# A conditioned GRU with residual: reset product in fp16 parts, candidate in 64-column halves, one seed for both gates

## The chip, the cores and the metric

One core of one Trainium2 chip runs the whole kernel. The metric is the device time of one execution in microseconds (us). Before the change it is 2313.37 us, the median of three runs (2312.4 to 2314.2).

## What is computed

A batch of 32 sequences of 512 time steps with 512 features goes through a GRU whose three gates get a constant term from a conditioning vector. Each new state is added to the input at that step.

```
xz, xr, xh = x @ W_z, x @ W_r, x @ W          # for every step, independent of the state
vz, vr, vh = cond @ C_z + b_z, cond @ C_r + b_r, cond @ C + b
step:  z  = sigmoid(xz_t + h @ U_z + vz)
       r  = sigmoid(xr_t + h @ U_r + vr)
       hh = tanh(xh_t + (r * h) @ U + vh)
       h  = (1 - z) * h + z * hh
out = x + h_t for every t
```

All arrays are fp32 with 512 x 512 weights. The 512 steps are a chain: step t needs the state of step t-1 twice in sequence, once for r and once more, through r, for hh.

## The kernel before, in words

**Layout.** A 32 x 512 tile (batch x features) lies as 128 partitions x 128 columns: partition block j of 32 partitions holds feature columns 128 j to 128 j + 127. VectorE's transpose in 32 x 32 blocks of such a tile gives the operand that TensorE loads as weights: 32 columns of it are the 32 batch rows for one of four groups q of 128 features. A product with a 512 x 512 matrix is four values of q times four column tiles j, 16 matmuls of 128 x 32 weights and 128 moving columns. The four of one q go to different column tiles of the array. An fp32 matmul shows as two records in the trace, each with its weight load.

**fp16 parts.** Where a product isn't done in fp32, both operands are scaled by a power of two and split in a high and a low fp16 part; three of the four products of parts are taken (`PARTS`). So it is with x @ W (`project`: 12 groups of four matmuls with 384 columns, all three gates at once) and h @ U_z (`update_product`, L253: 48 matmuls of 128 columns). h @ U_r and (r * h) @ U are fp32 (`product`, L225: 16 matmuls, 32 records each).

**One step on TensorE** (`step`, L299), in program order: the reset product R from the transposed state `h_t`, half by half as it comes; the update product U from `h_hi` and `h_lo`; in every fourth step a total of |x| (`total_x`), which gives the scale of a coming set of four steps; the first three groups (`BEFORE_C`) of the projection for step s+2; the candidate product C from `reset_t`, again half by half; the other nine groups. The projection has its own bank, one for even and one for odd steps. Waits, and so the order of everything, are written out by hand; each engine has its own program with semaphores.

**The seeds.** Before a product the cell in PSUM gets its starting value from VectorE: projection times scale plus constant term (`seed`, L441, one operation for each gate), and the matmuls add to it. For this the bits that make a matmul add must be set; six matmuls with zeros (L285) do that once. There are two sets of three cells, for even and odd steps. U_z is scaled, so the update cell's seed and constant are scaled as well and ScalarE's sigmoids take the scale back (`z_down`, `z_minus`, read from memory).

**The other engines in a step.** ScalarE: `h_hi` (L366), sigmoid for r (L368), the two sigmoids of z (L370, L371), tanh (L373), and at the end of three steps in four an operation on x for a later set: sum of |x|, fp32 scaling, high part (`sum_x`, `whole_x`, `high_x`). VectorE: seed of R for step s+1, `h_lo` (L523), reset times state and its transpose in two halves of 64 columns (L533, L535), seeds of the update and the candidate for s+1, transposition of x (L438), `taken` = z * hh (L549), new state and its transpose in two halves (L553, L555). GpSimd: `kept` = (1 - z) * h, low part of x, and the addition of x for the output. SyncE moves x and out in blocks of eight steps.

**Loops.** TensorE loops over sets of four steps and has the last 11 steps unrolled (L321 to L325). ScalarE, VectorE and GpSimd loop over 64 steps; ScalarE runs a one-element sigmoid at the head of its loop (L398), ahead of which stands the loading of its table.

**Ahead of the steps** the weights W_r, W_z, W_h and U_z are each measured, scaled and split (`top_of_w`, `rest_of_w`), the constant terms are computed with the C weights in fp32, and the loop starts when U_r and U_h have arrived too.

## Time and profile before

| | |
|---|---|
| median of three runs | 2313.37 us |
| time of the profiled execution | 2313.02 us |
| its span, first to last instruction | 2311.1 us |
| TensorE matmul busy | 2260.8 us, 98% |
| TensorE weight loads busy | 1885.7 us, 82% |
| VectorE busy | 1743.3 us, 75% |
| ScalarE busy | 1036.7 us, 45% |
| GpSimd busy | 686.8 us, 30% |
| chain that ended last, by engine | PE 96% |

PE is TensorE's matmul side and PEld its weight loads, which overlap it; DVE is VectorE, ACT ScalarE, POOL GpSimd. Times of rows are from the start of the span. A matmul's row gives its latency; matmuls are pipelined, so the pace is read from the starts of consecutive ones or from the pieces of the chain. A group's bracket gives the idle time of its engine ahead of it and what ended it.

### The profile page before, as it was taken

The page shows a single profiled execution, that of the slowest core. Times are in us where ns is not written, and L with a number is a line of the kernel's source. Part 1 is how long each engine was busy: PE and PEld are TensorE (multiplying, and loading weights), DVE is VectorE, ACT ScalarE, POOL GpSimd, SP SyncE. Part 2 cuts the span into 40 slices and gives each one's busy share as a digit, 9 for nine tenths or more (in the row PEclk, how much of TensorE's full clock was granted, in tenths as well). Part 3 has the DMA queues.
Part 4 walks back from the last instruction along what each step waited for, and adds up shares of the span by engine and source line. Part 5 has one row for each costly group of instructions (what it writes and reads, how often), then busy time and mean ns, then how long its engine had stood idle before and what let it go on. Part 6 is the DMA issues. An engine that isn't in the chain of part 4 may idle for free.

```text
span 2311.1 us, 185969 instructions
## 1 busy us (share of the span) xinstructions
PE 2260.8 (98%) x82966; PEld 1885.7 (82%) x82966; DVE 1743.3 (75%) x7717; ACT 1036.7 (45%) x3091; POOL 686.8 (30%) x1546
## 2 busy tenths in 40 slices
PE   3999999999999999999999999999999999999998
PEld 2888888888888888888888888888888888888887
DVE  5777777777777777777777777777777777777776
ACT  3444444444444444444444444444444444444443
POOL 0333333333333333333333333333333333333332
PEclk9999999999999999999999999999999999999999
DMA  9110110110110110101101101101101011011001
GB/s 192 33 37 22 33 37 19 37 37 19 37 37 19 37 34 21 37 23 33 37 19 37 37 18 37 37 19 37 34 22 37 24 32 37 19 37 37 19 19 22
DMA packets 145367, 78.25 MB, mean 34 GB/s; under 512 B 9024, under 2 KB 140608, under 8 KB 145216
## 3 DMA queue, kind: packets, MB, share of 16 engines
q1 hardware_dynamic: 145216, 76.84, 13.8%
q14 instruction: 131, 1.07, 0.2%
q8 instruction: 20, 0.33, 0.1%
HBM read 43.25 MB, written 33.55 MB: 33 GB/s over the span
## 4 chain that ended last, share of the span: by engine, by line
PE 96%; SPq 2%; issue 1%; DMA 1%; ACT 0%; DVE 0%; ACTq 0%; POOLq 0%; POOL 0%; DVEq 0%
PE p_bank L238 43%; PE banks L230 39%; PE banks L260 15%; SPq L136 1%; DMA u<-in_L_cond_U_dram 1%; SPq L131 0%; PE p_bank L246 0%; SPq L146 0%; SPq L139 0%; ACT h_hi L366 0%; ACT table L398 0%; ACTq L397 0%; ACT L398 0%; ACT gate_c L373 0%; POOLq L48 0%
## 5 line engine op out<-in xcount | busy, mean ns | idle before, releaser
L238 PE MATMUL p_bank<-w_hi,x_t 128*32 128x384 f16 x16384 | 1189.1, 327 | 3.6 <-DVE w_lo L465 3.5
L238 PE MATMUL p_bank<-w_lo,x_t 128*32 128x384 f16 x8192 | 712.1, 327 | 0.0
L238 PEld LDWEIGHTS p_bank<-w_hi,x_t 128*32 128x32 f16 x16384 | 482.6, 97 | 144.4 <-issue 4.0
L230 PE MATMUL banks<-u,h_t 128*32 128x128 f32 x16352 | 544.9, 274 | 5.8 <-DMA u<-in_L_cond_U_dram 4.1
L230 PE MATMUL banks<-u,reset_t 128*32 128x128 f32 x16352 | 541.6, 273 | 1.4 <-issue 0.9
L230 PEld LDWEIGHTS banks<-u,h_t 128*32 128x32 f32 x16352 | 411.4, 109 | 107.7 <-DVE h_t L555 93.6
L200 POOL TENSOR_TENSOR kept<-keep,state 128x128 f32<-128x128 f32 x512 | 234.4, 458 | 887.3 <-ACT keep L370 887.3
L230 PEld LDWEIGHTS banks<-u,reset_t 128*32 128x32 f32 x16352 | 428.5, 109 | 82.8 <-DVE reset_t L535 66.5
L443 DVE SCALAR_TENSOR_TENSOR banks<-p_bank,x_down,base 128x128 f32<-128x128 f32 x1536 | 478.4, 342 | 4.2 <-issue 3.8
L212 POOL TENSOR_TENSOR result<-x_nat,state 128x128 f32<-128x128 f32 x512 | 234.2, 457 | 723.0 <-DVE state L553 723.0
L533 DVE TENSOR_TENSOR reset<-gate_r,state 128x64 f32<-128x64 f32 x1024 | 209.3, 204 | 210.6 <-ACT gate_r L368 210.5
L366 ACT ACTIVATE h_hi<-h_t 128x128 f16<-128x128 f32 x512 | 158.3, 309 | 398.1 <-DVE h_t L555 398.1
L373 ACT ACTIVATE gate_c<-banks 128x128 f32<-128x128 f32 x512 | 141.9, 277 | 398.7 <-PE banks L230 398.7
L549 DVE TENSOR_TENSOR taken<-gate_c,gate_z 128x128 f32<-128x128 f32 x512 | 149.4, 292 | 185.0 <-ACT gate_c L373 185.0
L535 DVE STREAM_TRANSPOSE reset_t<-reset 128x64 f32<-128x64 f32 x1024 | 251.7, 246 | 37.5 <-DVE reset L533 1.7
L238 PEld LDWEIGHTS p_bank<-w_lo,x_t 128*32 128x32 f16 x8192 | 241.2, 97 | 47.3 <-issue 0.3
L555 DVE STREAM_TRANSPOSE h_t<-state 128x64 f32<-128x64 f32 x1024 | 251.2, 245 | 35.3
L370 ACT ACTIVATE keep<-banks,z_minus 128x128 f32<-128x128 f32 x512 | 188.1, 367 | 190.6 <-PE banks L260 190.6
L368 ACT ACTIVATE gate_r<-banks 128x128 f32<-128x128 f32 x512 | 141.8, 277 | 245.4 <-PE banks L230 245.2
L187 POOL TENSOR_TENSOR x_parts<-x_whole,x_parts 128x128 f16<-128x128 f32 (+1 forms) x509 | 237.0, 466 | 8.4 <-ACT x_parts L339 8.4
L553 DVE TENSOR_TENSOR state<-taken,kept 128x64 f32<-128x64 f32 x1024 | 208.5, 204 | 17.4
L260 PE MATMUL banks<-uz_hi,h_hi 128*32 128x128 f16 x8176 | 208.6, 219 | 0.5
(55 smaller groups left out, 1869.8 us busy)
## 6 DMA issues: line engine op xcount, KB each, us to landing
x_nat<-in_x_dram SPq DMA_DIRECT2D x256, 128.0 KB, 3.0
out_dram<-result SPq DMA_DIRECT2D x256, 128.0 KB, 2.7
w_stage<-in_L_cond_W_r_dram SPq DMA_DIRECT2D x4, 256.0 KB, 5.6
w_stage<-in_L_cond_W_z_dram SPq DMA_DIRECT2D x4, 256.0 KB, 8.4
w_stage<-in_L_cond_W_dram SPq DMA_DIRECT2D x4, 256.0 KB, 10.8
u<-in_L_cond_U_z_dram SPq DMA_DIRECT2D x4, 256.0 KB, 13.6
c_w<-in_L_cond_C_r_dram SPq DMA_DIRECT2D x4, 256.0 KB, 12.3
c_w<-in_L_cond_C_z_dram SPq DMA_DIRECT2D x4, 256.0 KB, 15.2
```

The costliest lines, as they stand in the source:

```text
L187: return nc.gpsimd.tensor_tensor(x_parts[k][:, part_of, 1], x_whole[k][:, part_of], x_parts[k][:, part_of, 0], ALU.subtract)
L200: nc.gpsimd.tensor_tensor(kept[:], keep[:], state[:, (tt - 1) % SLOTS], ALU.mult).then_inc(kept_ready, 1)
L212: nc.gpsimd.tensor_tensor(result[o][:, t], x_nat[j % BUFS][:, t], state[:, tt % SLOTS], ALU.add)\
L230: last = nc.tensor.matmul(out[part(j)], turned[:, part(q)], weights[:, q, cols(j)], start=first and q == 0, stop=q == Q - 1, skip_group_ch ...
L238: last = nc.tensor.matmul(p_bank[k][part(j), 0:G * N], x_t[:, c, part(q), a], w[b][:, :, q, cols(j)], start=f == 0, stop=f == GROUPS - 1, ...
L260: last = nc.tensor.matmul(out[part(j)], (h_hi, h_lo)[a][:, part(q)], uz[b][:, q, cols(j)], start=False, stop=q == Q - 1, skip_group_check= ...
L370: nc.scalar.activation(keep[:], cell(k, Z), ACT.Sigmoid, scale=z_minus[:]).then_inc(z_keep, 1)
L443: last = V.scalar_tensor_tensor(cell(k, g), p_bank[k][:, cols(g)], x_down[d][:, g:g + 1], base[:, g], ALU.mult, ALU.add)
L533: V.tensor_tensor(reset[:, half(a)], gate_r[:, half(a)], old[:, half(a)], ALU.mult).then_inc(reset_ready, 1)
L535: V.transpose(reset_t[:, half(a)], reset[:, half(a)]).then_inc(reset_t_ready, 1)
L553: V.tensor_tensor(new[:, half(a)], taken[:, half(a)], kept[:, half(a)], ALU.add).then_inc(h_ready, 1)
L555: V.transpose(h_t[:, half(a)], new[:, half(a)]).then_inc(h_t_ready, 1)
```

## The change

1. *Reset product in fp16 parts.* U_r is split like U_z (`ur_hi`, `ur_lo`). The product is 48 matmuls, taken by halves of the state: high parts of half 0 (two weight parts), low part of half 0, the same for half 1. `h_hi` and `h_lo` are computed in two halves each. The reset sigmoid runs in two halves and reads its scale from memory.
2. *Scales.* W_r and W_z share one scale, U_z and U_r another, W_h has its own. U_r is loaded before the biases, where it was loaded behind the C weights.
3. *One seed for both gates.* The cells of reset and update are in neighbouring banks and get one seed of 256 columns, behind the reset transposes. The candidate has one pair of banks for all steps, one for each half of its columns, seeded within its own step behind `h_lo` (`seed_c`).
4. *Candidate by halves of its output columns* (`candidate_product`): columns 0 to 63 of each block first, with one projection group between the two operand halves, then columns 64 to 127. Two groups of the projection lie ahead of it instead of three. Each half has its own tanh, `taken`, new state and transpose; VectorE's order is take 0, renew 0, take 1, turn 0, renew 1, turn 1.
5. *Waits and loops.* TensorE waits for the candidate's seed before the projection; GpSimd's output addition waits for the next step's `h_lo`. Step 1 on TensorE is unrolled ahead of the loop and waits for U_h only before its candidate product; the last 10 steps are unrolled. ScalarE's first four steps are unrolled, and its loop edge comes after every fourth step of a 64-step pass.

The diff, cut to its core:

```diff
-        banks = [ctx.enter_context(nc.psum_tensor(f"banks{k}", [P, G, BANK], f32)) for k in range(2)]
+        banks = [ctx.enter_context(nc.psum_tensor(f"banks{k}", [P, GATES, BANK], f32)) for k in range(2)]
+        c_bank = ctx.enter_context(nc.psum_tensor("c_bank", [P, HALVES, BANK], f32))
...
             load_weights(u[:, Z], U_z, s_u_in[Z])
+            load_weights(u[:, R], U_r, s_u_in[R])
...
             load_x(1, 1)
-            load_weights(u[:, R], U_r, s_u_in[R])
...
                 pool.wait_ge(h_ready, HALVES * (s + 1) if first or last else pool.snap(HALVES * s + HALVES))
+                if not (last and tt == STEPS - 1):
+                    pool.wait_ge(h_lo_ready, HALVES * (s + 2) if first or last else pool.snap(HALVES * s + 2 * HALVES))
...
+            def candidate_product(halves, between):
+                for a in range(HALVES):
+                    for h in range(HALVES):
+                        if a == 0:
+                            pe.wait_ge(*halves[h])
+                        for q in range(Q // HALVES * h, Q // HALVES * (h + 1)):
+                            for j in range(J):
+                                last = nc.tensor.matmul(c_bank[part(j), a, 0:N // HALVES], reset_t[:, part(q)],
+                                                        u[:, C, q, half_cols(j, a)], start=False, stop=q == Q - 1,
+                                                        skip_group_check=True)
+                        if (a, h) == (0, 0):
+                            between()
+                    last.then_inc(c_mm, 1)
...
+            def reset_product(out, halves):
+                passes = [(h, a, b) for h in range(HALVES) for a in range(2) for b in range(2 - a)]
+                for n, (h, a, b) in enumerate(passes):
+                    if b == 0:
+                        pe.wait_ge((h_hi_ready, h_lo_ready)[a], halves[h])
+                    for q in range(Q // HALVES * h, Q // HALVES * (h + 1)):
+                        for j in range(J):
+                            last = nc.tensor.matmul(out[part(j)], (h_hi, h_lo)[a][:, part(q)], ur[b][:, q, cols(j)],
+                                                    start=False, stop=n == len(passes) - 1 and q == Q - 1,
+                                                    skip_group_check=True)
+                return last
...
-                product(cell(k, R), h_t, u[:, R], halves=[(h_t_ready, a) for a in halves]).then_inc(r_mm, 1)
-                update_product(cell(k, Z), now).then_inc(z_mm, 1)
+                reset_product(cell(k, R), halves).then_inc(r_mm, 1)
+                update_product(cell(k, Z)).then_inc(z_mm, 1)
+                pe.wait_ge(c_seeded, now)
...
-                    project(k, (c + 2) % SET, 0, BEFORE_C)
-                product(cell(k, C), reset_t, u[:, C], halves=[(reset_t_ready, a) for a in halves]).then_inc(c_mm, 1)
+                    project(k, (c + 2) % SET, 0, BEFORE_C - 1)
+                if candidate_in is not None:
+                    pe.wait_ge(candidate_in, 16 * J)
+                def one_group():
+                    if fill:
+                        project(k, (c + 2) % SET, BEFORE_C - 1, BEFORE_C)
+                candidate_product([(reset_t_ready, a) for a in halves], one_group)
                 if fill:
                     project(k, (c + 2) % SET, BEFORE_C, GROUPS)
+            step(0, 1, True, s_u_in[C])
             with pe.Fori(0, SETS - 3) as m:
-                for tt in range(1, SET + 1):
+                for tt in range(2, SET + 2):
                     step(m, tt, False)
...
+                for a in range(HALVES):
+                    act.wait_ge(h_t_ready, HALVES * s + (a + 1) if first or last else act.snap(HALVES * s + (a + 1)))
+                    nc.scalar.activation(h_hi[:, half(a)], h_t[:, half(a)], ACT.Copy, scale=2.0 ** POW)\
+                        .then_inc(h_hi_ready, 1)
                 act.wait_ge(r_mm, now)
-                nc.scalar.activation(gate_r[:], cell(k, R), ACT.Sigmoid).then_inc(r_gate, 1)
+                for a in range(HALVES):
+                    nc.scalar.activation(gate_r[:, half(a)], banks[k][:, R, half(a)], ACT.Sigmoid, scale=gates_down[:])\
+                        .then_inc(r_gate, 1)
...
+                for a in range(HALVES):
+                    act.wait_ge(c_mm, HALVES * s + (a + 1) if first or last else act.snap(HALVES * s + (a + 1)))
+                    nc.scalar.activation(gate_c[:, half(a)], c_bank[:, a, 0:N // HALVES], ACT.Tanh).then_inc(c_gate, 1)
...
+            for tt in range(SET):
+                step(0, tt, False, True)
             with nc.Fori(0, PASSES - 1, engines=[act.engine], hint_back_edge=True) as i:
-                nc.scalar.activation(table[:], z_minus[:], ACT.Sigmoid)
-                for tt in range(STEPS):
+                nc.scalar.activation(table[:], gates_minus[:], ACT.Sigmoid)
+                for tt in range(SET, STEPS + SET):
                     step(i, tt, False)
...
+            def seed_gates(k, d):
+                V.scalar_tensor_tensor(banks[k][:, :, 0:N], p_bank[k][:, 0:GATES * N].rearrange("p (g n) -> p g n", g=GATES),
+                                       x_down[d][:, W_GATES:W_GATES + 1], base[:, 0:GATES], ALU.mult, ALU.add)\
+                    .then_inc(seeded, 1)
+            def seed_c(k, d):
+                V.scalar_tensor_tensor(c_bank[:, :, 0:N // HALVES], in_halves(p_bank[k][:, cols(C)]),
+                                       x_down[d][:, W_C:W_C + 1], in_halves(base[:, C]), ALU.mult, ALU.add)\
+                    .then_inc(c_seeded, 1)
...
+                for a in range(HALVES):
+                    dve.wait_ge(h_hi_ready, count(HALVES * s + (a + 1)))
+                    V.scalar_tensor_tensor(h_lo[:, half(a)], h_t[:, half(a)], 2.0 ** POW, h_hi[:, half(a)], ALU.mult,
+                                           ALU.subtract).then_inc(h_lo_ready, 1)
+                seed_c(tt % 2, m % 2)
...
+                take(0)
+                renew(0)
+                take(1)
+                turn(0)
+                renew(1)
+                turn(1)
```

## Rows read from the trace of the kernel before

**Rows 1.** The page's first part: busy time, share of the span, instructions.

```profile
PE 2260.8 (98%) x82966; PEld 1885.7 (82%) x82966; DVE 1743.3 (75%) x7717; ACT 1036.7 (45%) x3091; POOL 686.8 (30%) x1546
```

**Rows 2.** The chain of waits, 1001 to 1020: start us, us, what.

```profile
1003.52 0.05 PE p_bank L246 x7
...
1006.42 0.88 PE banks L230 x32
1007.30 0.67 PE banks L260 x48
1007.97 0.49 PE p_bank L238 x12
1008.45 0.87 PE banks L230 x32
1009.33 1.46 PE p_bank L238 x36
```

**Rows 3.** Timeline of one step: start us, us, engine, line, operation.

```profile
1007.36 0.28 ACT L368 ACTIVATE gate_r<-banks 128x128 f32<-128x128 f32 x1 [0.47 <-PE banks L230]
...
1007.67 0.22 DVE L533 TENSOR_TENSOR reset<-gate_r,state 128x64 f32<-128x64 f32 x1 [0.39 <-ACT gate_r L368]
...
1007.78 0.35 PE L238 MATMUL p_bank<-w_hi,x_t 128*32 128x384 f16 x4
...
1007.93 0.24 DVE L535 STREAM_TRANSPOSE reset_t<-reset 128x64 f32<-128x64 f32 x1
...
1008.01 0.37 ACT L370 ACTIVATE keep<-banks,z_minus 128x128 f32<-128x128 f32 x1 [0.37 <-PE banks L260]
```

**Rows 4.** Timeline of a late step without projection.

```profile
2298.81 0.24 DVE L535 STREAM_TRANSPOSE reset_t<-reset 128x64 f32<-128x64 f32 x1
...
2299.11 1.08 PE L230 MATMUL banks<-u,reset_t 128*32 128x128 f32 x32 [0.26 <-DVE reset_t L535]
```

**Rows 5.** Timeline: one-column fp32 matmuls, then the projection.

```profile
1003.35 0.22 PE L246 MATMUL p_bank<-x_sum,row_sum 128*32 128x1 f32 x8
...
1003.41 0.34 PE L238 MATMUL p_bank<-w_hi,x_t 128*32 128x384 f16 x4
```

**Rows 6.** Groups by line and form: busy us, mean ns, idle before.

```profile
L370 ACT ACTIVATE keep<-banks,z_minus 128x128 f32<-128x128 f32 x512 | 188.1, 367 | 190.6 <-PE banks L260 190.6
...
L366 ACT ACTIVATE h_hi<-h_t 128x128 f16<-128x128 f32 x512 | 158.3, 309 | 398.1 <-DVE h_t L555 398.1
...
L339 ACT ACTIVATE x_parts<-x_nat,x_up 128x512 f16<-128x512 f32 x128 | 112.1, 876 | 0.0
...
L398 ACT ACTIVATE table<-z_minus 128x1 f32<-128x1 f32 x7 | 1.4, 203 | 0.1
```

**Rows 7.** Timeline of a loop edge of ScalarE and VectorE.

```profile
333.00 1.28 ACT L398 ACT_TABLE_LOAD   x1 [0.37 <-issue]
...
334.40 0.29 ACT L366 ACTIVATE h_hi<-h_t 128x128 f16<-128x128 f32 x1
334.51 0.36 DVE L443 SCALAR_TENSOR_TENSOR banks<-p_bank,x_down,base 128x128 f32<-128x128 f32 x1 [0.63 <-issue]
...
334.75 0.23 PEld L260 LDWEIGHTS banks<-uz_hi,h_hi 128*32 128x32 f16 x16 [0.39 <-ACT h_hi L366]
```

**Rows 8.** Queues with instructions, all of them, 76 to 2250: packets, MB, share.

```profile
q14 instruction: 126, 1.03, 0.2%
```

**Rows 9.** The same from 2254 to 2304, queue q8.

```profile
q8 instruction: 13, 0.21, 1.9%
```

**Rows 10.** Windows of four looped and of 11 unrolled steps: busy (instructions), clock.

```profile
1001.80:1019.35 17.55, 17.55 (x656) 14.71 (x652) 13.46 (x61) 7.95 (x24) 5.36 (x12) 1.00 0.24 60
2254.10:2304.60 50.50, 47.25 (x1668) 40.29 (x1664) 33.70 (x150) 17.48 (x56) 13.03 (x29) 1.00 0.07 15
```

**Rows 11.** Waits from 2254 to the end: us, times, longest.

```profile
PEld banks L230 <- issue: 5.9, 13, 1.7
```

**Rows 12.** Timeline: TensorE's first step in the recurrence.

```profile
55.63 1.93 PE L230 MATMUL banks<-u,h_t 128*32 128x128 f32 x32 [4.11 <-DMA u<-in_L_cond_U_dram]
```

More of the change, by code:

```diff
@@ L279, in _ @@
                 pe.wait_ge(s_c_in[g], 16 * J)
-                product(cell(1, g), cond_t, c_w[:, g], first=True).then_inc(s_base_mm, 1)
-            pe.wait_ge(s_zeros, 1)
+                product(base_cell(g), cond_t, c_w[:, g], first=True).then_inc(s_base_mm, 1)
             pe.wait_ge(s_base, G)
-            for k in range(2):
-                for g in range(G):
-                    nc.tensor.matmul(banks[k][:, g], zeros[:, 0:P], zeros[:], start=True, stop=True).then_inc(s_bits, 1)
+            clear_bits(c_bank)
+            clear_bits(banks[1])
             pe.wait_ge(seeded, 1)
+            pe.wait_ge(c_seeded, 1)
             pe.sem_inc(r_mm, 1)
             pe.sem_inc(z_mm, 1)
-            pe.sem_inc(c_mm, 1)
+            pe.sem_inc(c_mm, HALVES)
             total_x(TOTAL_STEP % 2, 0, 0, 3)
@@ L293, in _, with step @@
             project(0, 2, 0, GROUPS)
-            pe.wait_ge(s_w_hi, G + 1)
-            pe.wait_ge(s_w_lo, G + 1)
-            for g in range(G):
-                pe.wait_ge(s_u_in[g], 16 * J)
-            def step(m, tt, last):
+            def step(m, tt, last, candidate_in=None):
                 s = m * SET + tt
@@ L351, in _ @@
             high_x(1)
-            for m, g in enumerate(SPLITS):
-                act.wait_ge(s_w_up, m + 1)
-                nc.scalar.activation(split_of(g, 0), stage_of(g), ACT.Copy, scale=w_up[:, g:g + 1]).then_inc(s_w_hi, 1)
+            for g in SPLITS:
+                k = SCALE_OF[g]
+                act.wait_ge(s_w_up, k + 1)
+                nc.scalar.activation(split_of(g, 0), stage_of(g), ACT.Copy, scale=w_up[:, k:k + 1]).then_inc(s_w_hi, 1)
+            nc.scalar.activation(table[:], w_up[:, 0:1], ACT.Sigmoid)
             act.wait_ge(x_in[1], 16 * J)
@@ L514, in more @@
                     return not (last and m + sets >= STEPS // SET)
-                ahead = (tt + 1) % 2, (tt + 1) // SET % 2
-                if not (last and tt == STEPS - 1):
-                    if t == SET - 1:
-                        dve.wait_ge(x_down_ready, count(now_m + 2))
-                    dve.wait_ge(projected, count(s + 2))
-                    seed(*ahead, (R,))
-                dve.wait_ge(h_hi_ready, now)
-                V.scalar_tensor_tensor(h_lo[:], h_t[:], 2.0 ** POW, h_hi[:], ALU.mult, ALU.subtract)\
-                    .then_inc(h_lo_ready, 1)
-                if t == POWER_STEP and more(2):
+                for a in range(HALVES):
[3 more added lines that the diff above has]
+                seed_c(tt % 2, m % 2)
+                if t == POWER_STEP and more(2):
+                    dve.wait_ge(projected, count(s + 2))
                     power_x(m % 2, p_bank[TOTAL_STEP % 2][:, G * N:G * N + 1], now_m + 2, count)
@@ L539, in step @@
                 if not (last and tt == STEPS - 1):
[L540 removed]
+                    if t == SET - 1:
+                        dve.wait_ge(x_down_ready, count(now_m + 2))
+                    dve.wait_ge(projected, count(s + 2))
+                    seed_gates((tt + 1) % 2, (tt + 1) // SET % 2)
                 if t == POWER_STEP and more(2):
```

175 lines of the change are left out of this document (100 added, 75 removed).

## The prediction

> **What bounds the kernel now.** I read the busy shares first: TensorE is busy 98% of the span, VectorE 75% [rows 1]. The reader is to see that only TensorE can be the bound by its own work. Next the chain of waits of a step: it stays on TensorE throughout, in five pieces: reset product R 0.88 us, update product U 0.67, three projection groups 0.49, candidate product C 0.87, nine projection groups 1.46, together 4.37 us; one step in four has the total of x besides, 0.05 [rows 2]. The mean step is thus 4.385, and 511 steps are 2241 of the 2311 us span. Then the order of time within a step: what must happen between the end of R and the start of C on the other engines, since this runs beside U and three groups [rows 3]. In these rows the first transpose of `reset` ends at 1008.17, and C starts at about 1008.27, when the three groups have issued (1007.78 + 0.49). So the chain through the engines is only some 0.04 us shorter than its cover once TensorE's reaction is added. The kernel is bound by TensorE, with a recurrence just under it.
>
> **The change, part by part.**
>
> *R in half precision.* Thirty-two fp32 records (0.88) become 48 fp16 matmuls of the shape of U's: 0.67. Saves 0.21 a step.
>
> *C in 64-column halves.* The 32 records of 128 columns become 64 of 64 columns. No row has that shape. The fp16 product of 128 columns starts 48 matmuls in 0.67, that is 0.056 us for each four (one per column tile), and the fp32 product of 128 columns 0.109 for each four [rows 2]. Half the columns of the latter are the stream of the former: 16 x 0.056 = 0.89, plus 0.02. Bounds: if halving saved nothing, 16 x 0.109 = 1.74; and no less than 0.87, since the same columns pass. I take 0.89, because the one-column fp32 matmuls lie far under it: eight start in 0.06, 0.03 for each four [rows 5], so neither issue nor weight load holds the pairs at 0.056.
> A rule speaks against this part. The Trainium skill (TensorE: Matmul & The Clock Gate, "Wait — 56ns, not 53.3ns?") has a floor of about 25 ns from one matmul's start to the next, however few columns. By it C would be 64 x 0.025 = 1.6. The trace has 14 ns in U and under 8 ns in the one-column rows, so it disagrees where matmuls go to different column tiles.
>
> *TensorE's own sum* is 0.67 + 0.67 + 0.33 (two groups) + 0.89 + 0.16 (the group moved into C) + 1.46 = 4.18, against 4.37.
>
> *The cover of the reset chain shrinks.* Two groups instead of three lie ahead of C. Cover after R: 0.67 + 0.33 = 1.00. The chain: ScalarE starts 0.23 after the last fp16 matmul's successor has started (1007.78 to 1008.01) [rows 3]; the half gate; 0.03; reset 0.23; 0.03; transpose 0.24; 0.06 to TensorE (2299.05 to 2299.11, a step in which TensorE really waits) [rows 4]. The half gate now has its scale from memory. Such an activation of 128 columns takes 0.367 and of one column 0.203 [rows 6]; without it 128 columns take 0.28 [rows 3]. Bounds 0.20 and 0.37; I take 0.30, midway in columns and a little up. Sum 1.12: TensorE waits 0.12 before every C (0.02 to 0.19 by the bounds). In the steps with the total the wait is 0.07. The transposed second half comes 0.38 after the first; C's first quarter and the group in between last 0.22 + 0.16, so it is just in time.
>
> *Step: 4.18 + 0.13 = 4.31.* Gain 0.075 a step.
>
> *Back half, hidden.* From C's start TensorE has 0.89 + 0.16 + 1.46 = 2.51 until the next R. First columns complete after 0.61; tanh of a half (as the gate without a scale, 0.28, less 64 columns: 0.22) starts at 0.84, second at 1.28 and ends at 1.50; `take(1)` starts at 1.53 and sits ahead of `turn(0)` on VectorE, which ends at 1.93; h_hi's half (0.309 for 128 columns [rows 6]; 0.24) and TensorE's reaction bring R's operand at 2.27. Slack 0.24. ScalarE's work on x sits between (it starts at 1.39; the longest takes 0.88 [rows 6]): at most 2.47, still inside. R's later operand halves (h_lo after VectorE's two short operations) come before TensorE needs them. If this cover went, each 0.1 over costs 51 us.
>
> *VectorE.* Three seeds become two: one of 256 columns, estimated 0.48, one of 128 at 0.35 (a seed takes 0.36 [rows 7]); two operations are split (h_lo, taken), about 0.08 each. Sum about level with before. The candidate's seed moves behind h_lo, beside the rest of R; the gates' seed behind the reset. Neither ends last: `take(0)` is ready at 1.09 after C's start and VectorE is free at 1.03. With both ends of the seed (0.36 to 0.72) the cost is 0 to 0.02 a step. GpSimd's new wait for h_lo delays its addition by 0.6 us of 4.3, with nothing behind it before `keep`.
>
> *Loop edges.* ScalarE's loop edge has a table load: load at 333.00, h_hi only at 334.40, and U waits 0.39 [rows 7]. The next h_hi is now R's own operand. Tanh's end to the load 0.37, load 1.28, 0.12, h_hi 0.24, 0.06: 2.07 after 1.50 is 3.57 against the 2.51 available, a wait of 1.05 at 6 edges, +6.3 (before about 0.3 each, inside its total). VectorE's edge shows 0.63 of "issue" ahead of a seed [rows 7]; now h_lo stands there: about 0.5 x 7 = +3.5. Together 10.
>
> *Instructions fetched.* TensorE's queue q8 brings code: 13 packets, 0.21 MB, while the last, unrolled steps ran 1,664 pairs [rows 9, 10], so 64 B an instruction and 256 in a packet; none in the whole loop, where q14 alone loads instructions, for other engines [rows 8]. Those 13 packets took 50.5 us, 3.9 each; without the 5.9 us in which TensorE stood for "issue" there [rows 11] it is 3.4. A step now has 208 pairs, was 160: 256 instructions are 2.6 us of work, less than a packet's 3.4 to 3.9. So where code is new, code sets the pace. The end: 10 unrolled steps, 3,990 instructions, 15.6 packets x 3.75 (nearer the end at which it stood) = 58.5 us instead of 43 of work. The start: 8.2 packets for the unrolled step and the loop's first pass, between 21.6 (work alone) and 32 (8.2 x 3.9); I take 27.5.
>
> **Sum**, from the start of step 1 (55.63) [rows 12] to TensorE's end (2304.6): before 2249. After: 27.5 + 124 passes x 4 x 4.31 (2138) + 10 + 58.5 = 2234, 15 less. The start itself stays: U_r comes ahead of the C weights and delays the base by some 4 us, but the first R no longer waits for U_h; I take 0, bounds -3 and +3. Span 2311.1 - 15 = 2296; the profiled execution's time is 1.9 over its span: 2298. It was 2313.0 before, 0.4 under the median.
>
> **The rivals.**
> - *Wait absent.* If the half gate costs 0.20 to 0.22, the wait before C is 0.03 and the step 4.22: 0.09 x 511 = 46 less, 2252. For: one-column gates take 0.203. Against: 128 columns take 0.367.
> - *Reset chain longer (slower).* At 0.367 for the half gate the wait is 0.19 and the step 4.38, no gain, and the edges and code (+25) are then on top: 2335. It decides from 0.06 us more anywhere between R's end and the transposed half. For: the chain was within 0.04 of its cover already. Against: halves of other operations are shorter here.
> - *The loop's code no longer stays (slower).* The body grows from 1,313 to about 1,697 instructions, 84 to 109 KB; the trace shows only that 84 KB stay. From its place in the program it touches seven 16 KB blocks and ends within a few instructions of an eighth. If the block at the head is lost on each pass, TensorE stands about 3 us (a packet, 3.4 to 3.9, less what is queued) at 124 edges: +370, 2668. The Trainium skill (Advanced Engine Details and Errata, "ISA Cache") gives TensorE 128 KB in lines of 16 KB, eight lines: by it seven blocks and the one fetched ahead just fit, and one more would not.
> - *A floor per matmul (slower).* If the starts of the short fp32 records and not their columns set the pace, halving saves nothing: C takes 1.74, 511 steps 434 us more, 2732. The one-column rows speak against it [rows 5]. By the skill's 25 ns (TensorE: Matmul & The Clock Gate) it would be 1.6, and 2660.
>
> **How the numbers follow.** Forecast 60%, own range 2275 to 2322 (half gate 0.26 to 0.33, packet 3.4 to 3.9). Wait absent 8%, longer chain 15%, code lost 14%, floor 3%. The range 2250 to 2345 holds the first three and leaves out the last two and some tails. What a measurement can tell is 0.2%, 4.6 us. Under 2308.7: 45 of the 60 and the 8, 0.53. Within: 9 and 3, 0.12. Above: 6, 12, 14 and 3, 0.35.
>
> **What would show it.** R's piece 0.67 and C's with its group 1.05; every step 4.31, the ones with the total too. TensorE idle 0.12 before C, released by `reset_t`, some 60 us in sum. No wait at R except at loop edges (about 1 us, ScalarE). q8 packets about 9 up to the loop's end and 15 behind it, none between; packets within the loop mean the code rival. R waiting on h_hi or h_lo in every step would make the prediction wrong, and so would a half gate far from 0.30.

## The result: slightly slower

| | before | after |
|---|---|---|
| median | 2313.47 us (8 runs, 2312.4 to 2315.6) | 2319.92 us (8 runs, 2319.1 to 2322.0) |
| span of the profiled execution | 2311.1 us | 2318.3 us |

The ratio after to before is 1.0028, 95% interval 1.0017 to 1.0039: 6.5 us slower, just beyond what can be told from no change. Forecast was 2298, faster. The time lies in the forecast's own range (2275 to 2322), with the other sign. One of the four executions of experiment 4 took 4600 us, the other three 2403 to 2405; it is not in that experiment's ratio.

The page's first part and its instruction queues, of the kernel after [rows 1, 8]:

```profile
PE 2241.4 (97%) x107502; PEld 1815.9 (78%) x107502; DVE 1799.7 (78%) x8226; ACT 1295.2 (56%) x4623; POOL 687.6 (30%) x1546
...
q8 instruction: 26, 0.43, 0.1%
```

TensorE has 24,536 more matmuls and is busy 19 us less; ScalarE has 1,532 more instructions and is busy 259 us more. Nothing but TensorE is near a bound. Next the chain of waits of one steady step after (start us, us, what), against [rows 2]:

```profile
1006.75 0.67 PE banks L298 x48
1007.42 0.67 PE banks L307 x48
1008.09 0.33 PE p_bank L270 x8
1008.42 0.38 PE c_bank L259 x16
1008.80 0.16 PE p_bank L270 x4
1008.96 0.67 PE c_bank L259 x48
1009.63 1.46 PE p_bank L270 x36
```

R has fallen from 0.88 to 0.67 as it should. But the candidate's first quarter, 16 matmuls, takes 0.38 in the chain where the next 48 take 0.67 (0.22 for 16): a wait hides in it. From the starts of the matmuls, as a median over some 410 steps, the pieces are 0.670, 0.670, 0.462, 0.248, 0.162, 0.672 and 1.462: 4.346 a step, against 4.375 before (means of all but the long steps: 4.346 after, 4.391 before). The timeline after shows the wait (start, length, engine, line, operation, in brackets the engine's idle time ahead and what ended it), against [rows 3]:

```profile
1007.24 0.41 PE L307 MATMUL banks<-uz_hi,h_hi 128*32 128x128 f16 x16
...
1007.47 0.52 ACT L429 ACTIVATE gate_r<-banks,gates_down 128x64 f32<-128x64 f32 x2 [0.80 <-PE banks L298]
...
1007.81 0.22 DVE L615 TENSOR_TENSOR reset<-gate_r,state 128x64 f32<-128x64 f32 x1 [0.56 <-ACT gate_r L429]
...
1008.07 0.24 DVE L617 STREAM_TRANSPOSE reset_t<-reset 128x64 f32<-128x64 f32 x1
...
1008.37 0.27 PEld L259 LDWEIGHTS c_bank<-u,reset_t 128*32 128x32 f32 x16 [0.34 <-DVE reset_t L617]
```

From U's first matmul to C it is 1.13 us, against a forecast of 1.12, and the cover is the forecast's 1.00. Now the whole run. I take the start of U in steps 6 and 501 as marks; the chain before and after, in that order:

```profile
79.96 0.67 PE banks L260 x48
...
2255.23 0.67 PE banks L260 x48
```

```profile
76.90 1.34 issue
...
81.19 0.70 issue
...
85.80 0.67 PE banks L307 x48
...
2246.85 0.67 PE banks L307 x48
```

After is 5.8 us late at step 6, 8.4 ahead at step 501, and 7.2 late at the end. So the loop did bring 14.2 us; the first steps took 6.0 of them, and the last eleven 15.6. Within the loop seven steps are long, six of them 64 apart by 1.44 to 1.63 each and one by 0.79, 9.9 in sum. Before has six long steps too, 64 apart, but by 0.23 to 0.29 only, 1.5 in sum. Without the long steps the gain is 495 x (4.391 - 4.346) = 22. The first long one after, against [rows 7]:

```profile
338.46 0.36 DVE L603 SCALAR_TENSOR_TENSOR h_lo<-h_t,h_hi 128x64 f16<-128x64 f32 x2 [1.65 <-issue]
...
338.74 0.29 PE L298 MATMUL banks<-ur_hi,h_lo 128*32 128x128 f16 x8 [1.33 <-DVE h_lo L603]
```

VectorE stands 1.65 us for its own instructions, and R stands with it. ScalarE's edge has no table load any more, only the small activation that is there to hold the table, and R doesn't wait:

```profile
355.36 0.20 ACT L463 ACTIVATE table<-gates_minus 128x1 f32<-128x1 f32 x1 [0.44 <-issue]
```

The end after: the chain with its pieces of "issue", then a window over the last ten steps (us, busy and instructions of PE, PEld, DVE, ACT, POOL, granted clock, DMA share, GB/s) against [rows 10], and the queue there against [rows 9]:

```profile
2269.47 0.70 issue
2270.17 0.68 PE banks L298 x34
...
2272.65 1.12 issue
...
2276.72 1.07 issue
```

```profile
2250.50:2312.30 61.80, 44.50 (x1988) 38.08 (x1984) 31.35 (x143) 20.87 (x78) 11.66 (x26) 0.95 0.07 13
...
q8 instruction: 16, 0.26, 1.9%
```

TensorE works 44.5 of 61.8 us. Of the other 17, the list of waits puts 15.8 down to "issue", and 1.5 to operands in the last steps. Sixteen packets of 256 instructions come meanwhile, so I read "issue" as waiting for code; experiment 5 tests it.

### The profile page after: what moved, and what is told of

It reads as the page before. It is cut to its first block, busy times and chain, and to the rows that moved or that the text cites. A ratio compares the mean times of both kernels' runs of the same rounds, so it can differ in the third digit from the quotient of the medians.

```text
span 2318.3 us, 238050 instructions
## 1 busy us (share of the span) xinstructions
PE 2241.4 (97%) x107502; PEld 1815.9 (78%) x107502; DVE 1799.7 (78%) x8226; ACT 1295.2 (56%) x4623; POOL 687.6 (30%) x1546
## 4 chain that ended last, share of the span: by engine, by line
PE 95%; issue 2%; SPq 1%; DMA 1%; DVE 0%; ACT 0%; DVEq 0%; POOLq 0%; POOL 0%
PE p_bank L270 43%; PE c_bank L259 23%; PE banks L298 15%; PE banks L307 15%; SPq L152 1%; DMA x_nat<-in_x_dram 1%; PE p_bank L279 0%; SPq L147 0%; SPq L163 0%; DVE taken L637 0%; DVE state L641 0%; ACT gate_c L436 0%; DVE h_t L645 0%; SPq L155 0%; DVE h_lo L603 0%
## 5 line engine op out<-in xcount | busy, mean ns | idle before, releaser
L259 PEld LDWEIGHTS c_bank<-u,reset_t 128*32 128x32 f32 x32704 | 506.7, 110 | 213.7 <-DVE reset_t L617 164.4
L259 PE MATMUL c_bank<-u,reset_t 128*32 128x64 f32 x32704 | 648.9, 221 | 9.4 <-issue 9.0
L429 ACT ACTIVATE gate_r<-banks,gates_down 128x64 f32<-128x64 f32 x1024 | 265.9, 310 | 426.0 <-PE banks L298 425.3
L298 PE MATMUL banks<-ur_hi,h_lo 128*32 128x128 f16 x8176 | 303.4, 219 | 9.2 <-DVE h_lo L603 8.4
L298 PE MATMUL banks<-ur_hi,h_hi 128*32 128x128 f16 x8176 | 303.4, 219 | 2.3 <-issue 1.2
L298 PE MATMUL banks<-ur_lo,h_hi 128*32 128x128 f16 x8176 | 303.5, 219 | 0.7 <-issue 0.7
L425 ACT ACTIVATE h_hi<-h_t 128x64 f16<-128x64 f32 x1024 | 251.9, 250 | 92.0 <-DVE h_t L645 58.3
L603 DVE SCALAR_TENSOR_TENSOR h_lo<-h_t,h_hi 128x64 f16<-128x64 f32 x1024 | 229.6, 225 | 71.3 <-ACT h_hi L425 21.7
L270 PEld LDWEIGHTS p_bank<-w_lo,x_t 128*32 128x32 f16 x8192 | 242.1, 97 | 50.8 <-issue 5.1
L637 DVE TENSOR_TENSOR taken<-gate_c,gate_z 128x64 f32<-128x64 f32 x1024 | 229.9, 225 | 40.0 <-ACT gate_c L436 15.6
L507 DVE SCALAR_TENSOR_TENSOR banks<-p_bank,x_down,base 128x256 f32<-128x256 f32 x512 | 235.9, 461 | 0.0
```

The costliest lines, as they stand in the source:

```text
L259: last = nc.tensor.matmul(c_bank[part(j), a, 0:N // HALVES], reset_t[:, part(q)], u[:, C, q, half_cols(j, a)], start=False, stop=q == Q - ...
L270: last = nc.tensor.matmul(p_bank[k][part(j), 0:G * N], x_t[:, c, part(q), a], w[b][:, :, q, cols(j)], start=f == 0, stop=f == GROUPS - 1, ...
L298: last = nc.tensor.matmul(out[part(j)], (h_hi, h_lo)[a][:, part(q)], ur[b][:, q, cols(j)], start=False, stop=n == len(passes) - 1 and q == ...
L425: nc.scalar.activation(h_hi[:, half(a)], h_t[:, half(a)], ACT.Copy, scale=2.0 ** POW)\
L429: nc.scalar.activation(gate_r[:, half(a)], banks[k][:, R, half(a)], ACT.Sigmoid, scale=gates_down[:])\
L507: V.scalar_tensor_tensor(banks[k][:, :, 0:N], p_bank[k][:, 0:GATES * N].rearrange("p (g n) -> p g n", g=GATES), x_down[d][:, W_GATES:W_GAT ...
```

## The experiments

Twelve kernels, all against the kernel before on the same chip. Ratios are to before with their 95% interval; after has 1.0028. Before's median was 2313.5 beside after and 2312.1 to 2313.4 beside the experiments, so a difference to after of 1 us or so says nothing. First the table by stretches, each from the starts of U in the profiled execution (start of U in step 1 to step 6; to step 501, with the sum of its long steps' excess in brackets and the mean of the others; to the end of the trace):

```
                      median   1 to 6   6 to 501 (long)  mean step  last 11
before                2313.5    22.4     2175.2 (1.5)      4.391      56.1
after                 2319.9    28.4     2161.1 (9.9)      4.346      71.7
four groups ahead     2277.8    29.5     2118.8 (10.3)     4.259      69.4
none between          2318.3    28.4     2160.5 (9.9)      4.345      69.5
gate without scale    2275.6    30.5     2117.2 (10.9)     4.255      68.7
candidate whole       2404.8    26.4     2257.7 (7.0)      4.547      60.9
longer loop           2303.5    29.4     2160.4 (9.9)      4.345      54.3
VectorE written out   2309.3    29.0     2150.5 (0)        4.345      70.5
R in fp32             2343.2    26.8     2194.0 (6.1)      4.420      61.0
before, longer loop   2310.2    23.6     2175.1 (1.5)      4.391      52.7
three edits           2249.3    29.5     2108.0 (0)        4.259      53.1
turn first            2332.1    30.8     2189.2 (0)        4.423      54.3
two seeds             2311.8    28.1     2154.1 (2.8)      4.346      68.6
three, two seeds      2252.7    30.8     2110.4 (0)        4.264      53.8
```

**1. Four groups ahead of the candidate.**

```diff
-    BEFORE_C = 3
+    BEFORE_C = 4
```

> Four of the twelve projection groups stand ahead of the candidate's product instead of three (one of the four still between its operand halves, eight behind it). Theory A (TensorE's 0.137 us of waiting per step in the changed kernel is for the first half of reset_t, which VectorE ends too late): the fourth group is 0.16 us of work that fills the wait, so the step falls from 4.346 to about 4.21 us, 496 steps bring 65 us, and the time is about 2255 us (2245 to 2270). The price: the part behind the candidate is 0.16 us shorter, so its slack of about 0.24 us falls to about 0.1; R should still not wait, save in steps with x's own splitting on ScalarE. Theory B (the period of the loop is set by the chain from the candidate back to R, which gets no shorter by a longer cover): the wait moves ahead of R, the step stays at 4.33 to 4.35 us and the time at 2312 to 2320 us.

2277.8 us, ratio 0.985 (0.983 to 0.987): 42 us less than after. The chain of a step, and TensorE's waits from 100 to 2200 us (us in total, times, longest):

```profile
1006.36 0.73 PE banks L298 x48
1007.10 0.67 PE banks L307 x48
1007.76 0.49 PE p_bank L270 x12
1008.25 0.23 PE c_bank L259 x16
```

```profile
PEld banks L298 <- ACT h_hi L425: 86.7, 374, 0.3
PEld c_bank L259 <- DVE reset_t L617: 69.6, 369, 0.2
```

The wait ahead of C is gone, 16 matmuls take 0.223. The kernel after has in the same stretch

```profile
PEld c_bank L259 <- DVE reset_t L617: 157.5, 481, 0.4
```

What stands here at 69.6 is the ordinary gap of the weight loads, since the matmuls behind it start without a break. Theory A holds in kind. It gave 65 us and 42 came. The whole 0.162 of C's place came back, but R now waits 0.025 before its first matmul and 0.036 inside: `h_hi`, 86.7 us in the waits. And in one step in four the total of x costs its 0.06, which the wait had hidden. That leaves 0.087 a step. The kernel after has no such row for `h_hi` there: its nine groups covered it.

What had cost C's first quarter 0.025 shows in the weight loads. Here the first one starts ahead of its matmul (this is a step with the total of x), where in the step of after shown above it starts with it:

```profile
1003.75 0.32 PEld L259 LDWEIGHTS c_bank<-u,reset_t 128*32 128x32 f32 x16
...
1003.84 0.40 PE L259 MATMUL c_bank<-u,reset_t 128*32 128x64 f32 x16
```

As medians over the steps: with a lead of 27 ns or more (this kernel) the quarter takes 0.223 us; with 14 ns (experiment 3, steps with the total) 0.235; with 2 ns (after, and the other steps of experiment 3) 0.247.

**2. None between the operand halves.**

```diff
-                    project(k, (c + 2) % SET, 0, BEFORE_C - 1)
+                    project(k, (c + 2) % SET, 0, BEFORE_C)
...
-                    if fill:
-                        project(k, (c + 2) % SET, BEFORE_C - 1, BEFORE_C)
+                    pass
```

> The third projection group is issued ahead of the whole candidate product and none between its operand halves; everything else as in the changed kernel. Theory A (two operand halves arrive 0.47 us apart; the group between them only moves 0.16 us of cover from the second half to the first): the wait ahead of the first half goes, a wait of 0.08 to 0.14 us for the second half of reset_t comes after the first 16 matmuls (0.22 us of work), and the step is 4.33 to 4.37 us: 2312 to 2325 us. Theory B (the second half is early by more than the group's 0.16 us, so the group between is misplaced): the wait of 0.137 goes with nothing in its place, the step is about 4.21 us and the time about 2255 us.

2318.3, ratio 1.0027 (1.0017 to 1.0037): no difference from after. The chain shows why:

```profile
1007.89 0.49 PE p_bank L270 x12
1008.38 1.05 PE c_bank L259 x64
```

C starts without a wait (0.49 for three groups is plain work), and its 64 matmuls take 1.05 instead of 0.89: the same 0.16 us, now inside. The two operand halves come 0.38 apart, and a quarter of C with a group is 0.22 + 0.16. So the placing of the third group is neutral. What is short is the sum of the cover.

**3. The half gate without its scale.**

```diff
-...ACT.Sigmoid, scale=gates_down[:])\
+...ACT.Sigmoid)\
```

> The reset gate's sigmoid on ScalarE is taken without its scale operand from memory (the kernel leaves out the scaling of the reset gate's argument, so its values are not the reference's). Theory A (the 0.310 us of a half gate stand in the chain from R's last matmul to reset_t and thus in TensorE's wait of 0.137): without the operand the half gate takes about 0.22 us, as the half of gate_c does (0.223), the wait falls by about 0.09 to 0.05 us, the step to 4.26 us, and the time by 44 us to about 2276 us. Theory B (the wait for reset_t is set by VectorE, which is still at seed_c when the gate comes, not by the gate): the wait stays above 0.12 and the time within 5 us of 2320.

2275.6, ratio 0.984 (0.982 to 0.985), as theory A had it to the microsecond. The group by form and the wait of the whole trace (after: 310 ns; 164.4 us):

```profile
L429 ACT ACTIVATE gate_r<-banks 128x64 f32<-128x64 f32 x1024 | 173.2, 221 | 425.0 <-PE banks L298 424.3 <-PEq L338 0.7
...
PEld c_bank L259 <- DVE reset_t L617: 119.0, 502, 0.3
```

An operand that costs 89 ns on an engine with 56% load costs 91 ns a step of the whole kernel, because it lies in the one chain that is not covered.

**4. The candidate whole.** Product, seed, tanh and `taken` in full width, three groups ahead.

```diff
-                candidate_product([(reset_t_ready, a) for a in halves], one_group)
+                product(c_bank[:, 0, 0:N], reset_t, u[:, C], halves=halves).then_inc(c_mm, 1)
...
```

> The candidate's product, seed, tanh and taken go back to the whole width of 128 columns, with three groups ahead and none between; R keeps its half-precision operand and both gates their one seed. Theory A (splitting the candidate by columns costs 0.03 to 0.05 us of TensorE per step but takes about 0.3 us out of the chain from C's end to the next R): the 64 matmuls take 0.87 us instead of 0.92, TensorE waits about 0.26 us ahead of R for h_hi, the step is about 4.43 us and the time about 2360 us. Theory B (the back half has 0.24 us of slack and the split there is worth nothing, its price of 0.05 is): the step is 4.28 to 4.32 us and the time 2290 to 2305 us.

2404.8, ratio 1.039 (1.037 to 1.042): slower than both. Theory A in direction, but 45 us more. The nine groups take 1.73 from the first one's start to R (0.27 of wait, as expected), and R itself takes 0.77 instead of 0.67, as its second operand half is late too; the chain leaves TensorE for ScalarE and VectorE:

```profile
1001.92 0.29 ACT gate_c L424
...
1002.23 0.30 DVE taken L625
...
1003.09 0.27 ACT h_hi L414
...
1003.40 0.94 PE banks L287 x48
```

So the half-precision R pays only with the candidate in halves (product, seed, tanh and `taken` were put back together, so which of them counts most stays open). One without the other makes a step 4.55, 0.16 more than before.

**5. TensorE's loop two passes longer.**

```diff
-            with pe.Fori(0, SETS - 3) as m:
+            with pe.Fori(0, SETS - 1) as m:
...
-            for s in range(SET * (SETS - 3) + 2, T):
+            for s in range(SET * (SETS - 1) + 2, T):
...
+                if last and (m, t) == (STEPS // SET - 4, WHOLE_STEP):
+                    act.sem_inc(x_summed, 2)
```

> TensorE's loop runs two passes further, so that 2 steps stand unrolled behind it instead of 10 (for it, ScalarE adds 2 to the semaphore of x's sums at the end, and two unused sums of x are made); all else as in the changed kernel. There the eleven last steps took 71.6 us from the update product on, against 56.0 before, 5.3 to 6.9 us for each of the 10 unrolled ones. Theory A (the unrolled steps wait for TensorE's instructions: 420 of them per step with the smaller matmuls against 324, at about 3.7 us for 256): 8 steps fall from 6.2 to 4.35 us, the time falls by 14 to 16 us to about 2305 us. Theory B (the last steps are slow because the supply of x and the other engines' last pass end there): the same 8 steps stay above 5.5 us and the time within 4 us of 2320.

2303.5, ratio 0.996 (0.994 to 0.998), 16.4 less than after: theory A. Moving eight steps into the loop changes none of their work. The same eight steps are 4.34 each. The chain at the place where after waited for "issue", and queue q8 from 2260 us on:

```profile
2271.07 0.67 PE c_bank L259 x48
2271.74 1.46 PE p_bank L270 x36
2273.20 0.67 PE banks L298 x48
```

```profile
q8 instruction: 3, 0.05, 0.5%
```

**6. VectorE written out.**

```diff
-            with nc.Fori(0, PASSES - 1, engines=[dve.engine], hint_back_edge=True) as i:
+            for i in range(PASSES - 1):
...
-                    return v if last else dve.snap(v)
+                    return v
```

> VectorE's program is written out for all 512 steps, without its loop of 64 steps; all else as in the changed kernel. There six steps, 64 apart, take 5.8 to 6.0 us instead of 4.35, with VectorE waiting 1.65 us for its own instructions ahead of h_lo. Theory A (the jump back to the loop's start costs VectorE this): the six long steps go, the time falls by about 9 us to about 2311 us. Theory B (VectorE's instructions are fetched as it goes in any case, and code that never jumps is fetched no faster): the long steps stay or spread, and the time is within 3 us of 2320, or longer if straight code is fetched more slowly than VectorE uses it.

2309.3, ratio 0.9986 (0.9976 to 0.9995): 10.6 less than after, and no step of the loop is long. Theory A: the jump is the cost, and straight code comes in time. The edit also takes the register arithmetic for the waits out of every step, but the other steps stay as they were (4.345 against 4.346). The seventh long step goes as well: it is the one from step 454 to 455, shortly behind the end of VectorE's loop (step 447).

**7. R in fp32 again**, with four groups ahead.

```diff
-                reset_product(cell(k, R), halves).then_inc(r_mm, 1)
+                product(cell(k, R), h_t, u[:, R], halves=[(h_t_ready, a) for a in halves]).then_inc(r_mm, 1)
...
```

> The reset product goes back to fp32 with h_t as its operand (32 matmuls; the result isn't scaled as its gate assumes, so its values are not the reference's), with four groups ahead of the candidate, one of them between the operand halves, as in the kernel that did away with the wait. Theory A (TensorE's work sets the step once the wait ahead of the candidate is covered): R costs 0.88 instead of 0.70, the step is 4.39 to 4.41 us against 4.26, and the time 2278 + 512 x 0.14 = about 2345 us, less some 8 us for shorter unrolled steps. Theory B (R's fp32 operand h_t is there about 0.4 us before h_hi and h_lo, and in that kernel R waits 0.09 us for those, so half precision brings less than its 0.21 us of matmuls): the step is 4.35 us or less and the time 2320 us or less.

2343.2, ratio 1.013 (1.012 to 1.015): theory A's 2345. The step is 4.420 against 4.259. Half precision is worth 0.16 of its 0.20 us with four groups ahead. C is not quite covered here: in the steps without the total its matmuls start without a break, but the weight loads just ahead of them wait for `reset_t`, and the first quarter takes 0.247 again:

```profile
1003.27 0.27 PEld L259 LDWEIGHTS c_bank<-u,reset_t 128*32 128x32 f32 x16 [0.20 <-DVE reset_t L620]
1003.27 0.43 PE L259 MATMUL c_bank<-u,reset_t 128*32 128x64 f32 x16
```

With 32 fewer instructions a step, the last eleven steps are 61.0 instead of 69.4.

**8. The kernel before with the longer loop.** The same two edits in its code (3 steps remain unrolled).

> The kernel before, with TensorE's loop two passes longer, so that 3 steps stand unrolled behind it instead of 11. There the eleven took 4.5 to 5.4 us, 4.75 on average, against 4.39 in the loop. Theory A (the unrolled code is fetched at about 3.7 us per 256 instructions, and 324 per step need 4.7 us): the time falls by 8 x 0.35 = 3 us, so the changed kernel gives away 12 us more on this stretch than the kernel before. Theory B (the end of the work is slow for another reason): no change, within 1 us.

2310.2, ratio 0.9989 (0.9979 to 0.9998): 2.8 less than before, where the same edit gave 16.4 to after. So the end of the changed kernel costs it 13.6 us that the kernel before doesn't pay. This is twice the 6.5 us by which the change lost.

**9. The three edits together** (1, 5 and 6).

> The three edits together: four groups ahead of the candidate, TensorE's loop two passes longer (2 steps unrolled at the end), VectorE written out without its loop. If the three are independent, 2319.9 less 42 (cover), 16 (tail) and 10 (VectorE's edges): about 2252 us. A tail step was slow by about 1.9 us in either kernel, an edge by 1.5. Rival: VectorE's straight code is slower in a shorter step, or the cover's gain and the edges' overlap: 2258 us or more.

2249.3 (5 runs, 2249.0 to 2251.4), ratio 0.973 (0.972 to 0.974): 63 us less than before on the same chip, and 69 less than after by the ratios. The parts were 42, 16 and 11, and add up. R's piece of the chain is 0.73 and that of C's first quarter 0.23, as in experiment 1.

**10. And the first half turned first.**

```diff
                 take(0)
                 renew(0)
-                take(1)
                 turn(0)
+                take(1)
```

> As the kernel with the three edits together, and VectorE turns the first half of the new state before it takes the second half (turn(0) ahead of take(1)). Once the candidate is covered, TensorE waits 0.02 us ahead of R for the first half of h_hi and 0.06 inside R. Theory A (the first half of h_hi is what is late): it comes about 0.1 us earlier, R's waits shrink by 0.03 us or more, and the time falls by 15 us or more, to about 2236 us. Theory B (the second half is what is late, since TensorE needs it only 0.34 us behind the first and it comes 0.38 us behind): turning first delays it by 0.1 us or more, R waits longer inside, and the time rises by 10 to 50 us.

2332.1, ratio 1.008 (1.007 to 1.010), 83 more than without it: theory B, and more than it said.

```profile
1000.91 1.30 PE p_bank L270 x32
1002.21 0.89 PE banks L298 x48
```

R starts no earlier (1.30 for eight groups) and takes 0.89 at the median instead of 0.70: it is the second half of the state that is late, and turning the first one sooner pushes it back.

**11. Two seeds for the gates.**

```diff
-                V.scalar_tensor_tensor(banks[k][:, :, 0:N], p_bank[k][:, 0:GATES * N].rearrange("p (g n) -> p g n", g=GATES),
-                                       x_down[d][:, W_GATES:W_GATES + 1], base[:, 0:GATES], ALU.mult, ALU.add)\
-                    .then_inc(seeded, 1)
+                for g in (R, Z):
+                    last = V.scalar_tensor_tensor(cell(k, g), p_bank[k][:, cols(g)], x_down[d][:, W_GATES:W_GATES + 1],
+                                                  base[:, g], ALU.mult, ALU.add)
+                last.then_inc(seeded, 1)
```

> The changed kernel with its one seed of both gates (256 columns, 0.46 us) taken apart again into two of 128 columns (0.35 each), at the same place on VectorE, so VectorE has 0.24 us more ahead of taking the candidate's first half. Theory A (behind the candidate nine groups leave 0.24 us of slack, as the prediction worked out, and VectorE was free 0.06 before the first half of the tanh came): the first h_hi comes 0.18 us later, still covered or nearly so, and the time is within 10 us of 2320. Theory B (the slack is smaller, as R's waits of 0.09 us with eight groups suggest: 0.16 less 0.09 is some 0.08 to 0.16): R waits 0.05 to 0.1 us a step and the time is 2340 to 2375 us.

2311.8, ratio 0.9994 (0.9985 to 1.0004): 8 less than after, as fast as before. Theory A on the step, which is 4.346 as after; what I didn't expect is the gain. It is in the loop, 7.0 us of it: the long steps have shrunk from 1.5 to 0.47 each. At the same place as after's 1.65 of "issue" this kernel has

```profile
337.49 0.36 DVE L604 SCALAR_TENSOR_TENSOR h_lo<-h_t,h_hi 128x64 f16<-128x64 f32 x2 [0.63 <-ACT h_hi L425]
```

So the jump's cost goes with VectorE's body, but not with its length alone. VectorE's idle time at the jump is 1.52 to 1.92 us at every edge of after and of experiments 1, 2, 3, 5 and 7, whose bodies have 16 instructions in most steps. It is 0.56 to 0.65 in before and in experiment 4, with 15, and at most 0.63 here, with 17. One instruction more and one fewer both make it cheaper. That it is where the body's start and end fall in what is fetched together is my reading. No run moved the body alone.

**12. Two seeds in the kernel with the three edits.**

> The same two seeds in the kernel with four groups ahead of the candidate, the longer loop and VectorE written out. Theory A (there R already waits in the steps that the back half sets, so each 0.1 us more on VectorE ahead of it counts in full): up to 0.18 us a step, 0.18 x 512 = 92 us, about 2330 to 2345 us. Theory B (VectorE's seed ends ahead of the tanh and only what lies beyond counts): 0.05 to 0.12 us a step, 2275 to 2310 us. No change from 2249 would mean that the one seed for both gates is worth nothing.

2252.7, ratio 0.974 (0.972 to 0.975), against 0.973 (0.972 to 0.974) with one seed. Neither theory; the step differs by 0.005, which is 2.4 us over the loop and lies within the intervals. So two seeds too end early enough for the tanh, and the step hardly asks for the one. Here, without a loop of VectorE, the single seed is worth 2 us or nothing; in the changed kernel, with its loop, it costs 8.

## Why the prediction was wrong

From the start of step 1 to TensorE's end it had 2234 us; 2256.7 were measured (55.92 to 2312.6), 22.7 more:

| term | forecast | measured | difference |
|---|---|---|---|
| five first steps | 27.5 | 29.0 | +1.5 |
| 496 steps of the loop | 2138 (4.31 each) | 2155.7 (4.346 each) | +17.7 |
| loop edges | 10 | 9.9 | -0.1 |
| ten unrolled steps | 58.5 | 62.1 | +3.6 |

- **The step that failed is "Step: 4.18 + 0.13 = 4.31".** Its first term was right: without waits the pieces are 0.670 + 0.670 + 0.325 + 0.223 + 0.162 + 0.670 + 1.462 = 4.18 (C from experiment 1). So were cover, 1.00, and chain, 1.13 for 1.12. The second was too small: the sum charged 0.126 for the wait, and it cost 0.162. Of the 0.036 between them, 0.011 is the wait itself (0.137) and 0.025 is what the sum left out: when the operand comes so late that the first weight load can't run ahead of its matmul, C's first quarter takes 0.248 instead of 0.223. Experiment 7 shows that this price goes with the late weight load, since there it is paid with no idle time of the matmuls. In the steps with the total of x TensorE idles 0.06 less, but the price and the step are the same. 0.036 us is small, but it is half of the gain that I forecast, and it comes 496 times.
- **That a wait would appear** was right, with its place and its chain. I treated it as a price of the change. Experiment 1 shows that it was a mis-set size beside it: two groups ahead where three were needed.
- **C in column halves** at 0.89, against 1.74 if halving saved nothing: 0.893 measured. No floor per matmul shows: 64 of them in 0.89 are 14 ns each.
- **The half gate** at 0.30: 0.310. Experiment 3 confirms both its price and that it counts in full. The rival with the wait absent gave 2252 for a half gate of 0.20 to 0.22. Experiment 3 has that gate (221 ns) and took 2275.6: a wait of 0.046 and the 0.025 stay, so that the step is 4.255 and not 4.22, and the rest is in the long steps and the two ends. Experiment 1, with no wait at C, took 2277.8 because the back half came up.
- **Back half** with 0.24 of slack: R waits nowhere after but at the edges, and VectorE's extra 0.24 in experiment 11 is covered. With one group fewer behind C (0.16) R's waits sum to 0.06 where no edge disturbs (experiment 9), so there was some 0.1 of slack in the half that comes second. I had worked out only the first.
- **Loop edges** agree in the sum by chance. ScalarE's table load, 6.3 of the 10, doesn't occur in the loop. Before ran its first sigmoid inside the loop, and the load stood ahead of it on each pass (seven of them, from 47.86 us on). After has a small sigmoid ahead of the steps as well (L412 of its code), and the only load but that at the start stands there:

```profile
42.32 1.28 ACT L412 ACT_TABLE_LOAD   x1
```

  The forecast took the load from before's edge and missed this line of the change. VectorE's edge, 3.5 in the forecast, took six times 1.5, and 0.8 more in the step behind its loop's end. Its 0.63 of "issue" [rows 7] was taken for what such an edge costs, when it was only what it cost with that body.
- **Code.** No packet of q8 from 85 to 2250 us, and none of the code rival's 370 us. Where code is new it sets the pace, as forecast: 3,990 instructions are 15.6 packets, in 62.1 us 4.0 each against the 3.75 taken. Experiments 1 and 2, with the same code there, took 59.9 and 59.8, 3.8 each; some 1.6 us of the difference is R and C of after's last step, which ran at the lower clock (below). Experiment 5 makes it a cause and not a coincidence. Where the steps have fewer instructions, fewer packets come and the ten steps are shorter: 13 in 50.8 us in experiment 4, 14 in 51.8 in experiment 7.
- **The sign.** By the forecast's own terms a gain of 42 in the loop (2138 against 2180 measured before; the 4.385 that the prediction took for before's mean step was 4.394 with the long ones) stood against some 27 of losses: edges 10, first steps 4 (27.5 against 23.3 from R of step 1 to R of step 6 before), last ten steps 12 (58.5 against 46.2). An error of 0.036 in a step of 4.31, under 1%, is 18 us and more than the difference of 15, and I gave three quarters of the forecast's weight to "faster". With a net so much smaller than either side it should have been nearer even.

## What to carry to other kernels

When work is made shorter that lies ahead of a wait, or moved out from in front of it, count the cover anew and move filler work until the chain is hidden; here one constant was worth 42 us, six times what the whole change had lost. A shorter matmul form is paid for in instructions, so code that runs only once (peeled and unrolled steps, the first pass of a loop) gets slower by the ratio of the counts where the arrival of code sets its pace; keep such steps few. And try a loop written out where its engine waits for "issue" at each turn.

## What the runs showed of the hardware

- 16 fp32 matmuls of 64 columns took 0.247 us from the first's start to the next group's when their first weight load started 2 ns ahead of its matmul (after, experiment 7), 0.235 with 14 ns, and 0.223 with 27 ns or more (experiment 1). It made no difference whether the matmuls had idled before (after, 0.137 us) or not (experiment 7).
- Halving the columns of fp32 matmuls halved the time from one start to the next: 64 of 64 columns in 0.893 us, 32 of 128 in 0.873.
- The scale operand from memory made the half gate 310 ns instead of 221; the tanh of the same shape without one is 223.
- The clock can be lower in the last step. That of after stands behind gaps of 0.96 and 1.30 us of "issue" and the chain through the other engines. Its R, 48 matmuls that elsewhere take 0.67, takes 1.47; the window there has a granted clock of 0.50, the lower level, where those just ahead have 1.00. Experiment 2, with gaps of 0.68 and 1.03 at the same places, has 1.00 to TensorE's end and 0.67 for this R. That the longer gaps for code brought the clock down is likely by this, but not shown: no run changed them alone. The rows of after:

```profile
2306.95 1.47 PE banks L298 x48
...
2298.50:2304.50 6.00, 3.91 (x170) 3.15 (x159) 2.95 (x14) 1.91 (x8) 0.91 (x2) 1.00 0.01 3
...
2306.90:2310.90 4.00, 2.96 (x108) 2.72 (x112) 1.48 (x8) 0.77 (x3) 0.46 (x1) 0.50 0.02 4
```

- VectorE's jump back cost at most 0.3 us in the step before, 1.5 at each of six after, 0.47 with one instruction more in a step (experiment 11), 0.6 with one fewer (experiment 4), and nothing written out.
